# A graph network on one core: half groups, pieces of x by truncation, and blanking scatters moved up

## The chip, the cores and the metric

The kernel runs on one core of a Trainium2 chip. The metric is the device time of one execution, in microseconds (us). Before the change it is 10419.15 us, the median of three runs (10417.22 to 10422.83).

## The reference

Four graph networks run one after the other on the same graph of N = 6250 nodes and E = 106250 edges, with D = 128 features; after each of them x becomes layernorm(x + network(x)). `src` and `dst` are the two ends of the edges, in an order that is known only at run time.

```
L0, 4 layers: agg = segment_sum(x[src], dst); h = (1+eps)*x + agg; linear, batchnorm, relu, ...; x = h + x_in
L1:           segment_sum(x[dst] @ W_T + edge_attr_64 @ T, src); relu(x @ W_S + that)
L2, 4 layers: msg = relu(x[src] + silu(edge_attr_16 @ We)); agg = segment_sum(msg, dst); mlp; layernorm
L3:           score = exp(clip(sum_heads(K[src]*Q[dst]*(edge_attr_128 @ WE)))); segment sums of V[src]*score and score by dst
```

So nine times a row of x is fetched for every edge and summed per target node, and once keys and values are. Everything is float32.

## The kernel before

**Order of the edges.** The 6250 nodes are 50 tiles of 125. Edges are sorted on the chip by the pair (tile of dst, tile of src). Four edges of one pair are a unit, 128 units of one tile are a group, and there are `GROUPS` = 272 groups (34 `TRIPS` of `Q` = 8). A tile's last group is filled up with blank units. `buckets` makes the histogram and the tables of where each pair starts, `scatter` writes the record of every edge (`rec`, 328 words) to its place in DRAM with indirect DMAs of POOL (L701), `metadata` reads back the node numbers and gives every unit its partner place in the order by the other end (L713, one indirect DMA for each group).

**Blanking.** In `setup` SP writes blank records over the part of `rec` that may stay unused (L532), then in `prepare` over the last group of each of 51 tiles (L548). Only after these have landed does POOL blank the last unit of each pair with 50 indirect DMAs (L688), and only after those does the main loop of `scatter` begin (L701).

**An edge pass** (`edges`, nine times: four of kind "sum", one "attr", four "msg") has two stages. In the row stage TensorE fetches the row of x of each edge as a product with a one-hot matrix. A group has 512 edges and one tile of nodes, whose place in SBUF is loaded into a register. x is held as three bfloat16 pieces, whose sum is x, so that a group takes 4 x 3 matmuls of 128 columns (L827). The registers are loaded eight at a time (L500), once for each trip:

```
at_ = tiles_of(PE_E, nat_row, i * Q, Q)
...
for j in range(UNIT):
    for k in range(3):
        ins = pe.matmul(ps[:, r, c], hots_t[0:NT, r, c],
                        big16[0:NT, ds(at_[q] + (2 * HT + k) * NODES_PAD, D)], ...)
```

DVE makes the one-hot matrix (L1481), ACT evicts the 512 rows (L1082), SP stores them in DRAM in unit order (L613). In the sum stage POOL gathers the 128 units of a group of the other order (L729, an indirect DMA), DVE makes another one-hot matrix (L1519), TensorE multiplies (L848, four products in float32, each of which is two matmul instructions in the profile; L851 are those of the 66 further features of "attr"), and DVE adds the result to the target tile of x (L1533, L1536), whose place is again a register loaded at the start of the trip. In a "msg" pass DVE adds the edge term to the gathered rows (L1526) and ACT applies relu (L1110) in between. Rings of four or eight buffers and semaphores order all of it.

**Pieces of x.** At the start of each pass ACT rounds x to bfloat16 (L1096), DVE subtracts (L1495), ACT rounds the rest (L1099), DVE subtracts again (L1498), in four parts; TensorE waits for all.

**Attention** (`attn`): POOL gathers keys and values with four indirect DMAs for each group (L739), TensorE fetches the rows of Q (L862) and makes the segment sums (L870), DVE multiplies and adds.

Between the passes stand the stages `linear`, `norm_linear`, `norm_apply`, `norm_out`, `layer_norm`, `to_t` and others, which are matmuls or transposes over 25 blocks of 250 nodes. Each stage begins when the one before has raised `stage_done`.

## Time and profile before

| what | value |
|---|---|
| median of the runs | 10419.15 us |
| profiled execution: its own time, its span | 10417.13 us, 10415.4 us |
| busy TensorE matmul, weight load | 7541.2 us (72%), 6497.3 us (62%) |
| busy VectorE (DVE) | 7092.3 us (68%) |
| busy GpSimd (POOL) | 4975.9 us (48%) |
| busy ScalarE (ACT) | 3677.0 us (35%) |
| DMA bytes, mean rate | 2371.77 MB, 228 GB/s |
| TensorE clock granted, mean | 0.817 |

The span runs from the first to the last instruction, the device time also has what lies around it (1.7 us here). Busy time is the union of an engine's instructions. Instructions of the engines' sequencers (register arithmetic, branches, waits, register loads, DMA issues) are not counted as busy; a "q" behind an engine's name marks them. A source line such as L827 is that of the kernel before. An idle time stands before the instruction that ended it, with what released it.

### The profile page before, as it was taken

The numbers are of one execution on the slowest core, as the hardware profiler recorded it, in microseconds if no ns is written. First come the engines' busy times: TensorE is split into PE (matmuls) and PEld (weight loads), VectorE is DVE, ScalarE is ACT, GpSimd is POOL, SyncE is SP. The second block draws the span as 40 slices with busy tenths as digits, with TensorE's granted clock in tenths as the row PEclk, the third lists the DMA queues.
The fourth block names the chain that finished last, engine by engine and source line by source line (L and its number), as shares of the span: only waits on it lengthen the run. The fifth ranks groups of instructions, "written<-read, shape, count | busy, mean of one in ns | idle before, by whom it ended". The sixth has DMA issues, their size and how long they took to land.

```text
span 10415.4 us, 240438 instructions
## 1 busy us (share of the span) xinstructions
PE 7541.2 (72%) x64204; PEld 6497.3 (62%) x64205; DVE 7092.3 (68%) x16971; ACT 3677.0 (35%) x7598; POOL 4975.9 (48%) x4705
## 2 busy tenths in 40 slices
PE   4799990388786886883689778777776885666664
PEld 3467660277675775773589776666765765555553
DVE  5577770366766766666556589789798797666664
ACT  0122220230612504304520454644645644444443
POOL 0777776336064072370035137056074173777772
PEclk7555555699898998996899899899898998666665
DMA  8766665997584874960699489598696894666666
GB/s 339 199 211 210 212 211 31 111 293 219 212 288 119 324 242 153 330 188 13 174 325 384 188 330 366 208 345 308 252 356 232 322 366 161 161 164 160 164 160 79
DMA packets 1747196, 2371.77 MB, mean 228 GB/s; under 512 B 516388, under 2 KB 1046151, under 8 KB 1746651
## 3 DMA queue, kind: packets, MB, share of 16 engines
q1 hardware_dynamic: 1292446, 1275.33, 39.0%
q0 software_dynamic: 318912, 1049.17, 31.2%
q10 hardware_dynamic: 135677, 45.42, 1.9%
q8 instruction: 65, 1.06, 0.0%
q14 instruction: 96, 0.79, 0.0%
HBM read 1485.10 MB, written 955.49 MB: 234 GB/s over the span
## 4 chain that ended last, share of the span: by engine, by line
PE 19%; DVE 9%; POOL 7%; issue 7%; ACT 4%; DMA 3%; SPq 2%; DVEq 2%; ACTq 0%; POOLq 0%
PE ps L848 8%; PE ps L827 7%; POOL big L739 7%; DVE gath L1526 3%; ACT gath L1110 3%; DMA big<-kv_table,src_at 2%; PE ps L851 2%; SPq L613 2%; ACT big L1245 1%; DVE onehot L1481 1%; DVE heads L1599 1%; DVE gath L1595 1%; ACT gath L1082 0%; DVE gath L1610 0%; PE ps L977 0%
## 5 line engine op out<-in xcount | busy, mean ns | idle before, releaser
L729 POOL DMA_INDIRECT gath<-msg_units,unit_at_d x2176 | 2329.4, 1071 | 3263.2 <-DMA msg_units<-gath 2579.2
L848 PE MATMUL ps<-onehot,gath 128*128 128x125 f32 x18224 | 2585.0, 287 | 620.6 <-ACT gath L1110 347.4
L848 PEld LDWEIGHTS ps<-onehot,gath 128*128 128x128 f32 x18224 | 2219.4, 193 | 977.3 <-issue 528.0
L827 PE MATMUL ps<-big,onehot 125*128 x29376 | 1795.4, 221 | 862.3 <-DVE onehot L1481 694.8
L827 PEld LDWEIGHTS ps<-big,onehot 125*128 125x128 bf16 x29376 | 1695.3, 98 | 965.3 <-issue 934.0
L1082 ACT ACTIVATE gath<-ps 128x512 f32<-128x512 f32 x2448 | 1393.2, 596 | 726.0 <-PE ps L827 571.5
L1519 DVE TENSOR_TENSOR onehot<-iota,node_d 128x500 f32<-128x500 f32 x2176 | 1464.4, 673 | 169.2 <-PE ps L848 109.9
L1481 DVE TENSOR_SCALAR onehot<-row_b,part 125x512 bf16<-125x512 uint8 x2448 | 1129.5, 482 | 606.4 <-PE ps L827 582.9
L739 POOL DMA_INDIRECT big<-kv_table,src_at x1088 | 1094.1, 1006 | 532.2 <-issue 295.6
L701 POOL DMA_INDIRECT rec<-big,idx_ring x832 | 974.5, 1171 | 279.9 <-issue 241.2
L1533 DVE TENSOR_TENSOR big<-big,ps 128x125 f32 x2448 | 685.4, 280 | 546.7 <-PE ps L848 375.8
L1110 ACT ACTIVATE gath<-gath 128x512 f32<-128x512 f32 x1088 | 685.5, 630 | 933.5 <-DVE gath L1526 933.5
L862 PE MATMUL ps<-big,weights 125*128 x2176 | 463.6, 380 | 414.8 <-DVE weights L1572 414.7
L1161 ACT ACTIVATE big<-ps,feats 128x250 f32 x125 | 54.2, 470 | 1987.7 <-PE ps L917 1987.7
L1526 DVE TENSOR_TENSOR gath<-gath,big 128x512 f32<-128x512 f32 x1088 | 742.3, 683 | 15.6 <-DMA gath<-msg_units,unit_at_d 15.6
L862 PEld LDWEIGHTS ps<-big,weights 125*128 125x128 f32 x2176 | 402.0, 276 | 478.4 <-issue 478.3
L870 PE MATMUL ps<-gath,onehot 128*125 128x136 f32 x2176 | 503.9, 401 | 122.2 <-DVE gath L1610 111.2
L1120 ACT ACTIVATE onehot<-iota,weights 128x125 f32<-128x125 f32 x1088 | 344.7, 388 | 650.7 <-PE ps L870 606.5
L1589 DVE TENSOR_TENSOR gath<-big,ps 128x512 f32<-128x512 f32 x272 | 186.9, 687 | 537.2 <-DMA big<-kv_table,src_at 531.3
L870 PEld LDWEIGHTS ps<-gath,onehot 128*125 128x125 f32 x2176 | 439.0, 288 | 181.4 <-issue 134.7
L729 POOL DMA_INDIRECT big<-rec,unit_at_s x136 | 131.1, 964 | 753.6 <-DMA rec<-gath 651.2
L807 PE MATMUL ps<-weights,big 128*128 128x128 f32 x1664 | 422.0, 433 | 93.9 <-ACT big L1044 82.5
(223 smaller groups left out, 9121.9 us busy)
## 6 DMA issues: line engine op xcount, KB each, us to landing
msg_units<-gath SPq DMA_DIRECT2D x2176, 256.0 KB, 2.3
big<-ea_units SPq DMA_DIRECT2D x1088, 256.0 KB
ea_units<-rec SPq DMA_DIRECT2D x16, 4352.0 KB, 53.2
rec<-gath SPq DMA_DIRECT2D x272, 256.0 KB, 6.2
big<-rec SPq DMA_DIRECT2D x272, 256.0 KB
big<-in_attr_t SPq DMA_DIRECT2D x208, 256.0 KB
rec<-big SPq DMA_DIRECT2D x1, 43296.0 KB, 152.4
gath<-msg_units,unit_at_d POOLq DMA_INDIRECT x2176, 5.3
```

What stands on the lines that cost most here:

```text
L701: pool.indirect_dma_start(rec, bass.IndirectOffsetOnAxis(ap=idx_ring[:, q, k:k + 1], axis=0), rec_r[:, q, k, :], None).then_inc(rec_out[q] ...
L729: pool.indirect_dma_start(att_slot(q) if way == "attr" else gath[:, q, :], None, units, bass.IndirectOffsetOnAxis(ap=unit_at[w][:, g:g + 1 ...
L739: pool.indirect_dma_start(kv_r[:, q, k, :], None, table["kv"], bass.IndirectOffsetOnAxis(ap=src_at[:, g * PER + k:g * PER + k + 1], axis=0))\
L827: ins = pe.matmul(ps[:, r, c], hots_t[0:NT, r, c], big16[0:NT, ds(at_[q] + (2 * HT + k) * NODES_PAD, D)], start=k == 0, stop=k == 2)
L848: ins = pe.matmul(ps[:, RING + r, 0:NT], x, hots[:, r, j, :], start=j == 0, stop=j == UNIT - 1)
L862: last = pe.matmul(ps[:, 6 + q % 2, k * P:(k + 1) * P], oht_r[0:NT, q % 2, k, :], big[0:NT, ds(at_ + RE * NODES_PAD, P)], start=True, stop ...
L870: last = pe.matmul(ps[0:NT, q, 0:SUMS_W], hots[:, q, k, :], vs_r[:, q, k, :], start=k == 0, stop=k == PER - 1)
L1082: act.activation(unit_ring[:, q, :, :], ps[:, q % RING, :].rearrange("p (k f) -> p k f", f=D), ACT.Copy).then_inc(evicted, 1)
L1110: act.activation(gath[:, q, :], gath[:, q, :], ACT.Relu).then_inc(msg_ready, 1)
L1481: dve.tensor_scalar(hots_t[0:NT, r, :].rearrange("p (j u) -> p j u", u=P), row_b[0:NT, k, q % RING * GSLOTS:(q % RING + 1) * GSLOTS] .rear ...
L1519: dve.tensor_tensor(hots[:, r, :, :], iota[:, 0:NT].unsqueeze(1).to_broadcast([P, UNIT, NT]), node[w][:, ds(g * UNIT, UNIT)].unsqueeze(2). ...
L1526: dve.tensor_tensor(gath[:, q, :], gath[:, q, :], ea_r[:, q, :], ALU.add).then_inc(msg_sum, 1)
```

## The change

Three things change at once.

**Half groups.** A group still has 128 units, but it is now made of two halves of 64 units (`HALF`), and each half has a tile of its own. Filling up to 64 instead of 128 leaves 248 groups (31 trips) for 272. Each group therefore has two tile numbers: register loads take 16 values for 8, the row matmuls take their tile by half, the sums of the two halves are separate matmuls of 64 rows into separate banks, and DVE adds twice, the second time after the first add has ended (`half_added`). In the "attr" pass the product is turned round (nodes on the partitions, 194 columns), so `to_t` is needed twice behind it. The order of the slots within a group changes too, so that stores go out as two runs for each unit pair, and `attn_prep` permutes two tables with matmuls.

**Pieces of x by truncation.** The upper two bytes of each float32 word are used in place as a bfloat16, with a step of two elements (`upper`). DVE makes the two rests by subtraction in five parts, and does it inside the stages that make x (`norm_out`, `layer_norm`); only the first pass cuts at its own start. ACT takes no part.

**Blanking.** POOL's 50 scatters now wait for the first blanking transfer alone, and for the transfers to the last (now half) groups only before the main loop. Blank units that fall into those go to spare rows.

```diff
-GROUPS = ((E + (UNIT - 1) * NTILES * NTILES) // UNIT + NTILES * (P - 1)) // P + 1
+HALF = P // 2
+HALVES = ((E + (UNIT - 1) * NTILES * NTILES) // UNIT + NTILES * (HALF - 1)) // HALF + 1
-TRIPS = -(-GROUPS // (2 * Q)) * 2
+TRIPS = -(-HALVES // (2 * Q))
...
+        def without_upper(dve, src, dst, k):
+            src, dst = (slice(b + k * FIFTH_W, b + (k + 1) * FIFTH_W) for b in (src, dst))
+            return dve.tensor_tensor(big[0:NT, dst], big[0:NT, src], upper[0:NT, src], ALU.subtract)
+        def cut(dve, src, k):
+            without_upper(dve, src * NODES_PAD, REST, k).then_inc(rest_made, 1)
+            cuts[0] += 1
+            dve.wait_ge(rest_made, cuts[0])
+            without_upper(dve, REST, LOW, k).then_inc(low_cut, 1)
@@ SP, prepare @@
-                    sp.dma_start(rec_units[ds(c, P), :], blank.rearrange("p j w -> p (j w)")).then_inc(last_blank, 16)
+                    sp.dma_start(rec_units[ds(c, HALF), :], blank[0:HALF, :, :].rearrange("p j w -> p (j w)"))\
+                      .then_inc(last_blank, 16)
@@ POOL, scatter @@
-                pool.wait_ge(last_blank, 16 * BKT)
+                pool.wait_ge(tail_blank, 16)
...
                 pool.wait_ge(unit_blank, 16 * NTILES)
+                pool.wait_ge(last_blank, 16 * BKT)
@@ TensorE, row stage @@
-                    at_ = tiles_of(PE_E, nat_row, i * Q, Q)
+                    at_ = tiles_of(PE_E, nat_row, i * (2 * Q), 2 * Q)
                         for j in range(UNIT):
-                            for k in range(3):
-                                ins = pe.matmul(ps[:, r, c], hots_t[0:NT, r, c],
-                                                big16[0:NT, ds(at_[q] + (2 * HT + k) * NODES_PAD, D)],
+                            for b in (NA * NODES_PAD, REST, LOW):
+                                ins = pe.matmul(ps[:, r, c], hots_t[0:NT, r, c], upper[0:NT, ds(at_[2 * q + j // 2] + b, D)],
                 laps(pe, TRIPS, rows_of)
+                pe.wait_ge(evicted, base + GROUPS)
@@ TensorE, sum stage @@
                         for j in range(UNIT):
+                            for h in range(2):
+                                p = slice(h * HALF, (h + 1) * HALF)
+                                if way == "attr":
+                                    x = att_slot(q)[p, j * REC + AT_EA:j * REC + AT_EA + D + AX]
+                                    ins = pe.matmul(ps[0:NT, (1 - h) * RING + r, 0:D + AX], hots[p, r, j, :], x, ...)
+                                else:
+                                    ins = pe.matmul(ps[:, (1 - h) * RING + r, 0:NT], unit_ring[p, q, j, :], hots[p, r, j, :], ...)
@@ DVE, sum stage @@
-                    at_ = tiles_of(DVE_E, sum_row, i * Q, Q)
+                    at_ = tiles_of(DVE_E, sum_row, i * (2 * Q), 2 * Q)
                             one_hots(g + 2, (q + 2) % RING, first and q < 2)
+                        add(g, 0, q % RING, at_[2 * q], first and q == 0)
                             message(i + (q + 2) // Q, (q + 2) % Q)
-                        add(g, q % RING, at_[q], first and q == 0)
+                        add(g, 1, q % RING, at_[2 * q + 1], False)
@@ DVE, layer_norm (norm_out alike, one sweep late) @@
                     last.then_inc(ln_fifth, 1)
+                    if then_cut:
+                        dve.wait_ge(ln_fifth, 5 * n["scaled"] + i + 1)
+                        cut(dve, b, i)
@@ the network behind the attr pass @@
+    do("to_t", AC, D, 0, RE)
+    do("to_t", HT, D, 0, AC)
```

## Rows read from the trace of the kernel before

**Rows 1.** The page's chain that ended last, shares of the span by line.
```profile
PE ps L848 8%; PE ps L827 7%; POOL big L739 7%; DVE gath L1526 3%; ACT gath L1110 3%; DMA big<-kv_table,src_at 2%; PE ps L851 2%; SPq L613 2%; ACT big L1245 1%; DVE onehot L1481 1%; DVE heads L1599 1%; DVE gath L1595 1%; ACT gath L1082 0%; DVE gath L1610 0%; PE ps L977 0%
```

**Rows 2.** Stages: length; PE, PEld, DVE, ACT, POOL busy; clock, DMA share, GB/s.
```profile
161.50:257.00 95.50, 0.00 (x0) 0.00 (x0) 0.62 (x2) 0.00 (x0) 0.00 (x0) 0.50 0.99 364
257.60:351.00 93.40, 31.19 (x122) 22.14 (x119) 22.43 (x74) 5.97 (x15) 51.89 (x50) 0.52 0.84 181
...
1991.00:2215.50 224.50, 195.00 (x3264) 186.78 (x3264) 161.60 (x406) 153.60 (x272) 0.00 (x0) 0.99 0.84 316
2219.00:2582.60 363.60, 304.42 (x2176) 264.96 (x2176) 238.28 (x545) 0.00 (x0) 275.48 (x272) 0.98 0.91 246
5024.70:5307.60 282.90, 234.73 (x3264) 199.60 (x3264) 164.05 (x405) 160.16 (x269) 0.00 (x0) 0.98 0.88 247
5321.00:5802.70 481.70, 478.64 (x4352) 478.23 (x4352) 290.28 (x817) 0.00 (x0) 259.92 (x270) 0.99 0.98 379
6148.00:6542.00 394.00, 315.86 (x2176) 265.89 (x2176) 378.94 (x812) 170.76 (x271) 301.29 (x270) 0.99 0.98 356
8831.60:10303.00 1471.40, 951.20 (x4316) 829.68 (x4317) 913.14 (x1886) 592.43 (x1630) 1093.72 (x1088) 0.68 0.66 157
```

**Rows 3.** Sequencer of TensorE in one trip of the row stage, by line.
```profile
L821 PEldq ALU_OP  x8: 32/32/36, 2064.9 to 2069.2; - x8
...
L823 PEldq EVENT_SEMAPHORE  x5: 51/51/51, 2066.8 to 2069.3; - x5
L823 PEldq ALU_OP  x3: 32/32/32, 2065.0 to 2066.2; - x3
...
L827 PEldq FUSED_REGOPS  x24: 46/46/46, 2065.1 to 2069.7; - x24
```

**Rows 4.** Register loads: count, ns min/median/max, first and last start, in four stretches.
```profile
L500 PEldq TENSOR_LOAD <-tile_at x24: 1123/1142/1168, 2044.0 to 2195.6; - x24
...
L500 DVEq TENSOR_LOAD <-tile_at x26: 595/599/615, 6210.7 to 6497.2; - x26
...
L500 PEldq TENSOR_LOAD <-tile_at x34: 1478/1938/1964, 8839.8 to 10257.8; - x34
...
L500 PEldq TENSOR_LOAD <-tile_at x2: 551/1258/1964, 8831.4 to 8839.8; - x2
```

**Rows 5.** POOL's indirect DMAs: a sum stage, attention.
```profile
L729 POOL DMA_INDIRECT gath<-msg_units,unit_at_d x272: 942/949/1455, 2219.7 to 2577.3; - x136
...
L739 POOL DMA_INDIRECT big<-kv_table,src_at x1088: 941/947/1477, 8831.6 to 10302.1; - x182
```

**Rows 6.** Timeline of DVE within a trip of a "msg" sum stage.
```profile
6307.24 0.27 DVE L1533 TENSOR_TENSOR big<-big,ps 128x125 f32 x1
...
6307.43 0.67 DVE L1519 TENSOR_TENSOR onehot<-iota,node_d 128x500 f32<-128x500 f32 x1
6308.02 0.68 DVE L1526 TENSOR_TENSOR gath<-gath,big 128x512 f32<-128x512 f32 x1
...
6308.62 0.27 DVE L1533 TENSOR_TENSOR big<-big,ps 128x125 f32 x1
```

**Rows 7.** Sequencer of TensorE on line L862, in 37 groups of attention.
```profile
L862 PEldq FUSED_REGOPS  x37: 46/46/46, 9311.9 to 9498.1; - x37
```

**Rows 8.** Timeline of DVE where one trip of a sum stage ends.
```profile
3009.59 0.28 DVE L1533 TENSOR_TENSOR big<-big,ps 128x125 f32 x1 [0.41 <-PE ps L848]
...
3010.80 0.68 DVE L1519 TENSOR_TENSOR onehot<-iota,node_d 128x500 f32<-128x500 f32 x1 [0.93 <-issue]
```

**Rows 9.** Timeline from the end of a stage to its pass's first matmul.
```profile
2669.03 3.02 ACT L1096 ACTIVATE big<-big 125x1632 bf16<-125x1632 f32 x2
...
2686.63 2.67 PE L827 MATMUL ps<-big,onehot 125*128 x23 [18.15 <-DVE onehot L1481]
```

**Rows 10.** Groups by line: name, count, busy us, mean ns, idle before.
```profile
L1767 DVE TENSOR_TENSOR big<-big,rows 125x1280 f32<-125x1280 f32 x5 | 7.5, 1493 | 0.2
```

**Rows 11.** Transposes of two `to_t` stages, one behind the other.
```profile
L934 PE MATMUL ps<-ident,big x100: 270/322/442, 4885.2 to 4900.8; 125*128 125x125 f32 x100
```

More of the change, by code:

```diff
@@ L159, in network @@
     do("attend")
-    do("norm_out", RE, HT, ACT.Identity, None)
+    do("norm_out", RE, HT, ACT.Identity, False)
     do("layer_norm", NA, D, None, None, False, None, "out", False)
@@ L353, in program @@
         base_u = of_small([BKT, 2, BKT])
-        quad, some, blank_f = (of_small([BKT, BKT]) for _ in range(3))
+        quad, some, blank_f, spare = (of_small([BKT, BKT]) for _ in range(4))
         groups_of = of_small([BKT, 2])
@@ L475, in do @@
                     names.append("io")
-                if kind == "norm_out" and args[3] or kind == "layer_norm" and args[6]:
+                if kind == "layer_norm" and args[6]:
                     names.append("io_fifths")
@@ L719, in edges @@
                 base, laps_before = n["edges"] * GROUPS, n["edges"] * TRIPS
-                units = rec_units if way == "attr" else msg_units
+                units = rec_units[0:UNITS + P, :] if way == "attr" else msg_units
                 if w == "s":
@@ L885, in attn, with attn_prep @@
                 sums(GROUPS - 1, RING - 1)
+            def attn_prep(n):
+                pe.wait_ge(turns_made, 1)
+                for t, v in enumerate((node_f, src_f)):
+                    v = v.rearrange("p (g i j) -> p g i j", i=2, j=2)
+                    for h in range(2):
+                        for i in range(2):
+                            last = pe.matmul(ps[:, 2 * t + h, 0:2 * GROUPS], turns[:, 2 * h + i, :], v[:, :, i, :],
+                                             start=i == 0, stop=i == 1)
+                last.then_inc(turned_at, 1)
             def attend(n):
@@ L1074, in load_rows, with keep_rows @@
                                   .partition_broadcast(P // 32)).then_inc(row_in[k], 16)
-                def keep_rows(i, first, last):
-                    for h in range(2):
+                def keep_rows(i, first, last, trips=2):
+                    for h in range(trips):
                         for q in range(Q):
@@ L1467, in spread, with row_hots @@
                     dve.stream_shuffle(words, words, [0] * 32).then_inc(row_spread, 1)
-                def row_hots(i, first, last):
-                    for h in range(2):
+                def row_hots(i, first, last, trips=2):
+                    for h in range(trips):
                         for q in range(Q):
@@ L1581, in add @@
                     dve.wait_ge(attn_sums, g + 1)
-                    ch.wait()
-                    a = big[0:NT, ds(at_ + HT * NODES_PAD, SUMS_W)]
-                    ch.mark(dve.tensor_tensor(a, a, ps[0:NT, q, 0:SUMS_W], ALU.add))
+                    for h in range(2):
+                        ch.wait()
+                        a = big[0:NT, ds(at_[h] + HT * NODES_PAD, SUMS_W)]
+                        ch.mark(dve.tensor_tensor(a, a, ps[0:NT, q, h * SUMS_W:(h + 1) * SUMS_W], ALU.add))
                 def times_q(g, trip, q):
@@ L1592, in times_eh @@
                 def times_eh(trip, q):
[L1593 removed]
+                    dve.wait_ge(eh_in[q], 32 * trip)
                     sch.wait()
@@ L1692, in norm_linear, with norm_out, pieces @@
                 bn_finish(n, g, b)
-            def norm_out(n, src, dst, func, tab):
-                with dve.Fori(0, NBLK) as j:
-                    dve.wait_ge(act_blk, n["applied"] * NBLK + j + 1)
-                    x = T(XT)[:, ds(j * BLK, BLK)]
-                    dve.tensor_tensor(x, x, T(dst)[:, ds(j * BLK, BLK)], ALU.add).then_inc(added, 1)
+            def norm_out(n, src, dst, func, then_cut):
+                base = n["blocks"] * NBLK
+                def pieces(i):
+                    dve.wait_ge(mm_free, base + SLOTS_PS * (i + 1))
+                    cut(dve, NA, i)
+                for i in range(SWEEPS):
+                    for j in range(i * SLOTS_PS, (i + 1) * SLOTS_PS):
+                        dve.wait_ge(act_blk, n["applied"] * NBLK + j + 1)
+                        x = T(XT)[:, j * BLK:(j + 1) * BLK]
+                        dve.tensor_tensor(x, x, T(dst)[:, j * BLK:(j + 1) * BLK], ALU.add).then_inc(added, 1)
+                    if then_cut and i:
+                        pieces(i - 1)
+                if then_cut:
+                    pieces(SWEEPS - 1)
             def conv(n, l):
```

276 lines of the change are left out of this document (150 added, 126 removed).

## The prediction

> **What bounds the kernel now.** I read the chain of waits by line, which names no single bound [rows 1], then the stages one by one [rows 2], because each has its own limit. The reader is to see four kinds.
> - The row stage takes 224.5 us for 272 groups, eight times (the "attr" one 282.9) [rows 2]. TensorE is busy 195.0 us of it. What sets the pace is TensorE's sequencer. In a trip of 8 groups it carries out 8 + 8 + 24 register and wait instructions between 2064.9 and 2069.7 [rows 3]: 39 intervals in 4.8 us, 0.123 us each, with the 96 weight loads and 96 matmuls in between. It then branches and loads eight registers, which takes 1142 ns [rows 4]. The loads come every (2195.6 - 2044.0)/23 = 6.59 us [rows 4], and 34 x 6.59 is the whole stage. The matmuls alone need 195.0/34 = 5.7 us a trip.
> - The "sum" sum stages (363.6 us) go at POOL's pace: 271 intervals in 357.6 us, 1.32 us for each gather [rows 5]. So does attention, 1470.5/1087 = 1.353 us, four for each group [rows 5]; metadata is one such DMA for each group and little else.
> - The "msg" sum stages (394 us, DVE busy 379 [rows 2]) go at DVE's pace: add to one-hot 0.19 us, one-hot to message 0.59, message to add 0.60, in all 1.38 [rows 6], and (6497.2 - 6210.7)/25 = 11.46 us a trip [rows 4].
> - The "attr" sum stage has DMA share 0.98 at 379 GB/s and TensorE 478.6 of 481.7 us busy [rows 2]: both are full, with 4352 matmuls at 0.110 us.
>
> **The change part by part.** All sums are made against the profiled execution, 10417.13 us, 2.0 under the median of the runs; terms are rounded to 1 us.
>
> *Row stages.* Groups fall from 272 to 248, trips from 34 to 31. But the tile of slots 0 and 1 is no longer that of slots 2 and 3. In a trip there are 24 fused register instructions on the line of the matmuls [rows 3], one for each different address and not one for each of the 96 matmuls: three pieces x 8 groups. Attention's four products on one tile also have one for each group, 37 in 186 us [rows 7]. With two tiles a group has six addresses, so 24 more instructions a trip. At 0.123 us [rows 3] that is 2.95 us. Bounds: nothing, if the compiler reuses the registers, and 0.15 us each, 3.6 us. I take the measured mean, because the three that stand already are of the same kind in the same place. The load of 16 registers isn't in the trace. At an aligned start the number counts little: two cost 551 ns on TensorE, eight cost 599 on DVE [rows 4]. Bounds are nothing and, with attention's 8 at a shifted start for 1938 ns, 0.24 us for each, 16 x 0.24 - 1.14 = 2.7 us [rows 4]. I take one more short access, 0.55 us. Trip: 6.59 + 2.95 + 0.55 = 10.09 us; stage: 31 x 10.09 = 313 us, 88 more than 224.5, eight times: +704. "attr": 313 for 282.9 us, +30. DVE (161.6 busy) and ACT (153.6) stay under that [rows 2]. The stores have twice the runs at half the length; with a DMA share of 0.84 now and a slower pace they are covered. The rows of x are read with a step of four bytes: bounds nothing and, as with the float32 passes at 0.110 us against 195.0/3264 = 0.060 [rows 2], 12 x 0.11 = 1.32 us a group, 10.6 us a trip, 0.5 over the sequencer's 10.09 (+140 in nine stages). I take nothing. TensorE's new wait for the last eviction has the sum stage behind it, which waits for the stores of the same rows: nothing.
>
> *"sum" sum stages.* POOL: 248 x 1.32 = 327 us. DVE in a trip: eight one-hots to first add, 0.60 each, eight first adds to second, which wait for the end of the first (0.28 and some 0.08 for the release), seven second adds to the next one-hot at 0.19, and the end of the trip, now 1.21 us [rows 8], with 0.55 more for the load: 4.8 + 2.9 + 1.4 + 1.8 = 10.9 us, 337 us for 31. That is a little more than POOL's, so DVE takes the bound: with the 5 us that the stage has around the gathers 342 us, -22 each, -88.
> The matmuls are 16 of 64 rows where 8 of 128 rows stand, alternating between the upper and the lower half of the array and between two banks. If the halves run side by side, TensorE needs what it needs now, 304.4/272 = 1.12 us a group [rows 2]. No row shows two such halves; the bound on the other side is one after the other, 16 x 0.110 = 1.76 us a group (rival 2). I take side by side, since nothing in the operands ties one half to the other. The Trainium skill (TensorEngine Tiling (Array Packing), Key Properties) says that tiles of the array load weights and multiply in parallel, which leaves the sum as it is; no trace here shows it.
>
> *"msg" sum stages.* The first add moves between one-hot and message, where its end is hidden, so it costs its issue, 0.19 us [rows 6]: a trip is 11.46 + 8 x 0.19 + 0.55 = 13.5 us, 31 are 419 us, +25 against 394, four times: +100. The fewer groups don't pay for the second add.
>
> *"attr" sum stage.* DMA-bound: each group gathers the same bytes, 481.7 x 248/272 = 439, -42. TensorE: 8 passes of 194 columns at 0.110 x 194/125 = 0.171, 1.37 us a group, if the halves run side by side.
>
> *Attention.* POOL-bound: 24 x 4 x 1.353 us = -130. DVE's busy 913 of 1471 us covers the second add (248 x 0.3) and the longer load. SP has one more issue a group, with 5.4 us for three. *Metadata:* at the same price 24 x 1.353 = -32.
>
> *Pieces of x.* Before each pass 17.6 us go by from the stage's end to the first matmul [rows 9]. Afterwards two subtractions of 1280 columns stand there, 1.49 us each [rows 10], then the spreading and the first one-hots. But the cuts weigh on DVE in the stages before: 10 x 1.49 = 15 us. In `norm_out` and in `layer_norm` with weights DVE gets full and gives some back: -8 (three) and -12 (three); without weights it is idle enough: -15 and -17. The first pass keeps its cut: -1. Together -93. Without the cover it would be 8 x 17.6 less 8 x 15, -21.
>
> *Blanking.* The transfers of the last groups take 95.5 us, the scatters 93.4 us behind them [rows 2]. Side by side, with half the bytes in the first (at 364 GB/s 47 us), the scatters start at 161.5 and end after 93 us at best and 93 + 47 at worst. POOL's issue takes 66 of the 93, so part of the others' bytes fits in: I take 107, which is -83 (bounds -97 and -49).
>
> *New stages.* Two `to_t`, of the size of those that take 15.6 us and their eviction now [rows 11]: +16. The permutation in `attn_prep`: 16 float32 passes of 496 columns, 0.110 x 496/125 = 0.44 us, and four copies: 7 + 3 us, and up to twice the first at the clock of 0.50 that TensorE has after idling, as at 161.5 us [rows 2]: +13 with a wait.
>
> **Sum.** +704 + 30 - 88 + 100 - 42 - 130 - 32 - 93 - 83 + 16 + 13 = +395, so 10417 + 395 = 10812, and 10815 as a run's time.
>
> **Rivals.**
> 1. *Faster: the addresses cost nothing.* The compiler or the queue of TensorE hides the 24 added instructions. For it: the matmuls need only 5.7 of the 6.59 us. Against it: the sequencer's instructions fill the trip without a gap [rows 3]. The rows would take 31 x 6.59 = 204 us (-20 each, "attr" -25): 10417 - 339 - 185 = 9893; with the 0.55 us for the load 10047. It decides where the nine row stages lose less than the other terms gain, 339/9 = 38 us: below (224.5 + 38)/31 = 8.47 us a trip.
> 2. *Slower still: the half matmuls queue.* 1.76 us a group. The "sum" stages take 248 x 1.76 + 5 = 441 (+99 on my 342, four times), "msg" 441 (+22, four times), "attr" 16 x 0.171 = 2.73 us, 678 (+239): 10812 + 723 = 11535. For it: the "attr" stage now shows 16 passes a group at just this pace. Against it: those fill all 128 rows.
> 3. *Slower still: each loaded register costs 0.24 us*, as at the shifted starts [rows 4]. Rows: 2.15 us more a trip, 31 x 9 times, 600. DVE: 16 x 0.24 - 0.60 - 0.55 = 2.7 us a trip, 31 x 8 times, 670. That is 12080. Against it: the aligned loads of eight. The Trainium skill (Runtime: NRT & Kernel Launch, Instruction fetch mechanics) has some 200 ns for each register even in bulk; attention's loads agree (0.24 us), the aligned ones don't (599 ns for eight).
>
> **How the numbers follow.** Forecast 0.56, rival 1 0.20, rival 2 0.16, rival 3 0.08. The forecast's own range is 10400 to 11250: below, 0.095 us an instruction and no price for the load; above, 0.15 us, the load doubled and the step of four bytes paid. Over all cases 9900 to 11500 holds rival 1 and part of rival 2, and leaves out 0.08 + 0.10. Faster by over 0.2% (about 21 us, what a measurement of this kernel can tell): 0.20 and the low end of the forecast, 0.23. Within it: 0.03. Slower: 0.74.
>
> **What would show it.** Row stage: 48 fused register instructions a trip on the line of the matmuls, trips of some 10.1 us for 6.59, TensorE waiting for its sequencer; rival 1 has 24 of them or 6.6 us. Sum stage: matmuls of the two halves starting together, 342 us for 363.6; rival 2 has 0.11 us between all starts. Loads of 16: near 1.7 us on TensorE, or 3.8. "msg": DVE full, 13.5 us a trip. Attention: 1341 us. First scatter at 162 us, main loop at 268. First matmul of a pass 4 to 9 us behind the stage. Wrong as a whole is the prediction if the row stages come out under 262 us each.

## The result

The changed kernel takes 11272.36 us, the median of four runs (11264.59 to 11281.23), where the kernel before takes 10418.18 on the same chip: a ratio of 1.082, 95% interval 1.0807 to 1.0833. It is slower by 854 us. I had forecast slower by 396; the forecast's own range ended at 11250, the one over all cases at 11500. The sign and several of the mechanisms were right, the size was less than half of it.

I read the stages first, since each has its own limit. This is the view by stages of the changed kernel, with the columns of [rows 2]: the blanking scatters; the blanking that was still to land; a "sum" row stage and its sum stage; the "attr" row and sum stages; a "msg" sum stage; attention.
```profile
164.10:225.00 60.90, 0.00 (x0) 0.00 (x0) 0.00 (x0) 0.00 (x0) 45.72 (x50) 0.50 0.99 175
225.00:348.50 123.50, 10.53 (x43) 8.45 (x44) 9.54 (x31) 2.99 (x6) 0.00 (x0) 0.50 0.82 176
2734.10:3064.90 330.80, 269.54 (x2976) 232.78 (x2976) 155.09 (x369) 147.45 (x247) 0.00 (x0) 0.83 0.56 196
3068.50:3430.90 362.40, 291.00 (x3968) 252.11 (x3968) 270.23 (x745) 0.00 (x0) 235.48 (x248) 0.95 0.78 225
5343.60:5728.40 384.80, 287.24 (x2976) 240.74 (x2976) 161.18 (x370) 148.13 (x248) 0.00 (x0) 0.82 0.55 166
5737.00:6163.80 426.80, 372.11 (x3969) 319.88 (x3969) 336.50 (x1241) 0.00 (x0) 236.92 (x248) 0.99 0.98 391
6616.00:7073.90 457.90, 323.65 (x3968) 281.21 (x3968) 398.50 (x989) 155.96 (x248) 245.72 (x246) 0.89 0.88 279
9827.00:11153.00 1326.00, 852.56 (x3931) 744.26 (x3932) 899.97 (x1959) 540.21 (x1486) 977.81 (x992) 0.68 0.67 159
```
TensorE and DVE are both busy for a smaller share in the row and msg stages than before: neither is full, so something between their instructions has grown. The granted clock has fallen with it: 0.99 of full speed in a row stage before [rows 2], 0.83 now, which is 2.4 GHz for two thirds of the time and 1.2 for the rest, while the pause at the end of a trip has grown from 0.90 to 1.93 us (below).

The terms of my sum against the two profiled executions (span 10415.4 and 11266.5 us), each measured from matmul to matmul of the stages, so that nothing is left over:

| term | forecast | measured |
|---|---|---|
| eight row stages | +704 | +849 |
| "attr" row stage | +30 | +97 |
| four "sum" sum stages | -88 | -14 |
| four "msg" sum stages | +100 | +233 |
| "attr" sum stage | -42 | -56 |
| pieces of x, with the two `to_t` | -77 | -88 |
| blanking, up to the end of the scatter | -83 | -1 |
| metadata | -32 | -40 |
| attention and the rest | -117 | -129 |
| sum | +395 | +851 |

**A row trip.** The timeline of TensorE in a row stage, first before, then changed; a line is a run of matmuls without a gap, and in brackets stands the pause ahead of it.
```profile
2099.80 4.07 PE L827 MATMUL ps<-big,onehot 125*128 x70
2104.77 5.70 PE L827 MATMUL ps<-big,onehot 125*128 x96 [0.90 <-ACT gath L1082]
```
```profile
2099.71 5.69 PE L858 MATMUL ps<-big,onehot 125*128 x66
2107.29 8.76 PE L858 MATMUL ps<-big,onehot 125*128 x96 [1.89 <-issue]
2117.98 6.20 PE L858 MATMUL ps<-big,onehot 125*128 x68 [1.93 <-issue]
```
The 96 matmuls of a trip are one line, and in the pause ahead of it stands the register load. So a trip is 5.70 + 0.90 before and 8.76 + 1.93 now. Both parts have grown. These are the loads at the ends of the same trips, before and then changed (the first of each starts at 2103.3 and at 2105.5):
```profile
L500 PEldq TENSOR_LOAD <-tile_at x2: 1140/1144/1147, 2103.3 to 2109.9; - x2
```
```profile
L515 PEldq TENSOR_LOAD <-tile_at x2: 1413/1415/1417, 2105.5 to 2116.1; - x2
```
Before, the load started 0.6 us ahead of the end of the last matmul (2099.80 + 4.07 = 2103.87), so that half of it was covered. Now it starts 0.1 us behind that end (2099.71 + 5.69 = 2105.40), and all of it stands in the pause. The load itself is only 0.27 us longer.

The sequencer's instructions of one such trip, and the register loads of the row stage and of a msg sum stage, in the changed kernel:
```profile
L852 PEldq ALU_OP  x7: 32/32/32, 2011.9 to 2018.3; - x7
```
```profile
L858 PEldq FUSED_REGOPS  x48: 64/64/64, 2011.0 to 2019.3; - x48
```
```profile
L515 PEldq TENSOR_LOAD <-tile_at x26: 1404/1425/2436, 1997.5 to 2266.7; - x26
```
```profile
L515 DVEq TENSOR_LOAD <-tile_at x31: 1096/1101/1124, 6618.7 to 7056.8; - x31
```
**Where a msg trip ends.** The timeline of DVE in the changed kernel, to hold against [rows 6]:
```profile
6690.83 0.28 DVE L1576 TENSOR_TENSOR big<-big,ps 128x125 f32 x1
6691.02 0.68 DVE L1560 TENSOR_TENSOR gath<-gath,big 128x512 f32<-128x512 f32 x1
6691.63 0.28 DVE L1576 TENSOR_TENSOR big<-big,ps 128x125 f32 x1
6693.12 0.68 DVE L1553 TENSOR_TENSOR onehot<-iota,node_d 128x500 f32<-128x500 f32 x1 [1.22 <-issue]
```
Inside a trip a group takes 1.58 us, 0.20 more than before, which is the 0.19 of the forecast. At the end of the trip DVE stands still for 1.22 us, and TensorE then has no work for 1.7 us. In most trips one slow group of matmuls follows, here the first of the second line (timeline of TensorE, same stage):
```profile
6680.70 1.16 PE L883 MATMUL ps<-onehot,gath 64*128 64x125 f32 x16 [1.73 <-DVE onehot L1553]
6682.28 3.44 PE L883 MATMUL ps<-onehot,gath 64*128 64x125 f32 x32 [0.42 <-ACT gath L1147]
6686.11 1.16 PE L883 MATMUL ps<-onehot,gath 64*128 64x125 f32 x16 [0.39 <-ACT gath L1147]
```
A group is 16 half matmuls in 1.16 us, and two groups 1.58 us apart should end 2.7 us after the first one's start, not 3.44. The first took 1.80 us at a granted clock of 0.50, which is 1.2 GHz, the group ahead of it 1.16 us at 0.97 (the same columns as above):
```profile
6680.70:6681.90 1.20, 1.16 (x16) 0.97 (x16) 1.20 (x4) 0.38 (x1) 0.81 (x1) 0.97 0.78 215
6682.30:6684.10 1.80, 1.80 (x16) 1.80 (x18) 1.55 (x4) 0.63 (x1) 0.79 (x1) 0.50 0.85 241
```
DVE then waited 0.65 us for it. Trips without such a group take 14.0 us, the others 14.7. The 1.16 us also settle rival 2: 16 half matmuls one behind the other at 0.110 us would take 1.76. In the trace the matmuls of the two halves start in pairs, 0.007 us apart, and the pairs every 0.111 us.

**The "attr" row stage.** What the engines waited for in it (total us, times, longest):
```profile
DVE onehot L1520 <- PE ps L858: 217.2, 200, 3.2
ACT gath L1124 <- DMA rec<-gath: 206.7, 208, 2.5
PEld ps L858 <- issue: 116.4, 122, 2.3
```
ACT waits for the landing of stores, at a DMA share of 0.55. The stores aren't slow (2.2 us from issue to landing): SP issues them late, two a group at 0.80 us each, one behind the other, since a half group's rows to `rec` need a transfer of their own. That is 12.85 us a trip, which the stage shows from its seventh trip on; the first ones take 10.7, as in the other row stages.

### The profile page after: what moved, and what is told of

Its sections match the earlier page's. It is cut to its first block, busy times and chain, and to the rows that moved or that the text cites. A ratio compares the mean times of both kernels' runs of the same rounds, so it can differ in the third digit from the quotient of the medians.

```text
span 11266.5 us, 268085 instructions
## 1 busy us (share of the span) xinstructions
PE 7933.5 (70%) x75296; PEld 6635.5 (59%) x75297; DVE 7279.9 (65%) x18698; ACT 3412.1 (30%) x7120; POOL 4463.7 (40%) x4369
## 4 chain that ended last, share of the span: by engine, by line
PE 18%; DVE 9%; issue 9%; POOL 6%; ACT 3%; SPq 3%; DMA 3%; DVEq 2%; ACTq 0%; POOLq 0%
PE ps L858 10%; POOL big L770 6%; PE ps L883 6%; SPq L639 3%; DVE gath L1560 2%; ACT gath L1147 2%; DVE big L1576 2%; DMA big<-kv_table,src_at 2%; DVEq L515 1%; DVE big L1572 1%; ACT gath L1124 1%; DVE onehot L1553 1%; DVE big L1573 1%; ACT big L1279 0%; DMA big<-rec 0%
## 5 line engine op out<-in xcount | busy, mean ns | idle before, releaser
L760 POOL DMA_INDIRECT gath<-msg_units,unit_at_d x1984 | 1985.8, 1001 | 4585.0 <-DMA msg_units<-gath 3404.1
L858 PE MATMUL ps<-big,onehot 125*128 x26784 | 2441.3, 250 | 1000.2 <-issue 495.1
L883 PE MATMUL ps<-onehot,gath 64*128 64x125 f32 x31744 | 2430.5, 300 | 886.7 <-DVE onehot L1553 421.8
L858 PEld LDWEIGHTS ps<-big,onehot 125*128 125x128 bf16 x26784 | 2093.3, 112 | 1351.1 <-issue 1076.3
L883 PEld LDWEIGHTS ps<-onehot,gath 64*128 64x128 f32 x31744 | 2104.6, 203 | 1212.5 <-issue 439.5
L1553 DVE TENSOR_TENSOR onehot<-iota,node_d 128x500 f32<-128x500 f32 x1984 | 1338.3, 675 | 314.6 <-PE ps L883 238.5
L1576 DVE TENSOR_TENSOR big<-big,ps 128x125 f32 x3968 | 1107.8, 279 | 249.6 <-PE ps L883 104.7
L770 POOL DMA_INDIRECT big<-kv_table,src_at x992 | 977.8, 986 | 528.3 <-issue 278.7
L1560 DVE TENSOR_TENSOR gath<-gath,big 128x512 f32<-128x512 f32 x992 | 679.6, 685 | 27.0 <-DMA big<-ea_units 19.2
L1506 DVE STREAM_SHUFFLE row_b<-row_b 128x512 int32<-128x512 int32 x558 | 406.8, 729 | 0.0
```

What stands on the lines that cost most here:

```text
L760: pool.indirect_dma_start(att_slot(q) if way == "attr" else gath[:, q, :], None, units, bass.IndirectOffsetOnAxis(ap=unit_at[w][:, g:g + 1 ...
L770: pool.indirect_dma_start(kv_r[:, q, k, :], None, table["kv"], bass.IndirectOffsetOnAxis(ap=src_at[:, g * PER + k:g * PER + k + 1], axis=0))\
L858: ins = pe.matmul(ps[:, r, c], hots_t[0:NT, r, c], upper[0:NT, ds(at_[2 * q + j // 2] + b, D)], start=b == NA * NODES_PAD, stop=b == LOW)
L883: ins = pe.matmul(ps[:, (1 - h) * RING + r, 0:NT], unit_ring[p, q, j, :], hots[p, r, j, :], start=j == 0, stop=j == UNIT - 1)
L1553: dve.tensor_tensor(hots[:, r, :, :], iota[:, 0:NT].unsqueeze(1).to_broadcast([P, UNIT, NT]), node[w][:, ds(g * UNIT, UNIT)].unsqueeze(2). ...
L1560: dve.tensor_tensor(gath[:, q, :], gath[:, q, :], ea_r[:, q, :], ALU.add).then_inc(msg_sum, 1)
```

## The experiments

Two of the four chips of these runs have slower POOL transfers, for every kernel alike (the kernel before takes 10401 and 10408 us on two, 11130 and 11222 on the others), so each ratio is against the kernel before on its own chip, and across chips I compare only the row stages, which hold no POOL transfer: the kernel before has them at 223 to 226 us on both kinds (e12). e1, e5, e9 and e12 are single executions.

### One tile for both halves (e1)

```diff
-at_ = tiles_of(PE_E, nat_row, i * (2 * Q), 2 * Q)      # DVE's sum stage alike
+at_ = tiles_of(PE_E, nat_row, i * Q, Q)
-... upper[0:NT, ds(at_[2 * q + j // 2] + b, D)]
+... upper[0:NT, ds(at_[q] + b, D)]
```

> Left out: the second half of a group takes the tile of another group, in the row stages and in the adds, so that a trip loads 8 registers for 16 and a group has 3 addresses for 6; all matmuls, adds and transfers stay. Theory (the sequencer's address instructions and the register loads set the time): per group of a row stage 3 fused register instructions at 0.143 us apart and 0.2 us for the rest, 0.63 to 0.66 us, with 1.85 us at the end of the trip some 7.1 us a trip for 10.72, so a row stage of 220 us for 331. In the msg sum stages the idle time of DVE at the end of a trip falls from 1.22 to some 0.3 us and with it TensorE's slow group goes (clock back over 0.97): 8 x 1.58 + 0.4 = 13.1 us a trip for 14.7, 406 us for 456. The sum sum stages go from 359 to about 332 us, where POOL's gathers (1.32 us) take over. Rival (the rows of x read at a step of four bytes, or TensorE's lower clock, set the pace): the row trip stays above 9.5 us. Rival for the sum stages (the second add's wait itself costs): msg trip stays above 14.2 us.

Measured: 10251.16 us, where the kernel before takes 10408.33 there. Row stages 222 to 243 us, msg sum stages 421 us, sum sum stages 331 us, a msg trip 13.3 us. That is 157 us under the kernel before, where the change is 854 over it: the loads and the second half's addresses together cost the change some 1010 us, and without them it would be a gain. The step of four bytes and the wait of the second add stay in this run, so they are not the cause of the loss. The run doesn't part the loads from the addresses. The "attr" row stage stayed at 380.1 us: it isn't paced by addresses.

### Three-step addresses (e2)

```diff
-dve.tensor_scalar(tiles_i[:, 2:4, :], ..., float(D), ...)
+dve.tensor_scalar(tiles_i[:, 2:4, :], ..., float(2 * D), ...)
-upper[0:NT, ds(at_[...] + b, D)]
+big16[0:NT, ds(at_[...] + (2 * b + 1), 2 * D)].rearrange("p (d t) -> p d t", t=2)[:, :, 0]
```

> The tile addresses are kept doubled in the table, so that a fused register instruction of the row stage holds three steps (add, multiply, add) for five; their number stays 48 a trip. Theory (the sequencer sets the row stages): each instruction takes 46 ns for 64 and they stand 0.124 us apart for 0.143, so a trip takes 10.72 - 48 x 0.019 = 9.8 us, a row stage 304 us for 331, eight of them -216 us; the attr one stays near 380 (another limit). Total near 11055 us. Rival (the step of four bytes or the clock of 0.84 sets the pace of the matmuls): row trip within 0.1 of 10.7, total 11270.

Measured: 11147.55 us, ratio 1.0713 (1.0682 to 1.0744). The instructions went to 46 ns and the matmuls of a trip to 7.89 us, but the pause grew, so that a row stage came to 313 to 317 us and not 304. From the same timeline and the list of register loads:
```profile
2106.48 7.89 PE L859 MATMUL ps<-big,onehot 125*128 x96 [2.33 <-issue]
```
```profile
L516 PEldq TENSOR_LOAD <-tile_at x30: 1397/1870/2411, 1949.0 to 2247.0; - x30
```
The same load now takes 1.87 us for 1.43: it isn't a fixed price, and half of what the addresses gave it took back. The granted clock was 0.84, as in the changed kernel (0.83), and the matmuls of a trip still took 0.87 us less: in this stage the sequencer sets the pace, not the lower clock.

### Blanking from 128 partitions (e3)

```diff
-sp.dma_start(rec_units[ds(c, HALF), :], blank[0:HALF, :, :].rearrange("p j w -> p (j w)"))
+sp.dma_start(rec[ds(c * UNIT, HALF * UNIT), :].rearrange("(p j) w -> p (j w)", j=2),
+             blank[:, 0:2, :].rearrange("p j w -> p (j w)"))
```

> The blanking of the last half groups writes the same bytes from 128 partitions of SBUF (two records each) and not from 64 (four records each). Theory (a transfer out of 64 partitions gets about half the rate: 17.1 MB at some 180 GB/s here, where full groups went at 364 GB/s before): the engines' time is 47 us for these and some 80 to 93 for the scatters, so the main loop of the scatter starts at 290 to 305 us for 336, -30 to -45 us of the whole. Rival (many writes beside scatters, or writes to DRAM as such, go at 180 GB/s whatever the source): it starts within 5 us of 336.

Measured: 11215.42 us, ratio 1.0778 (1.0747 to 1.081). The main loop of the scatter starts at 319.7 us for 348.5 (the 336 of the expectation was the first work of the other engines; POOL itself started later), so 29 us come from here; of the other 28 us of the difference 10 stand in the kernel before too (10408 us on this chip for 10418), and the rest is spread over the stages. The bytes up to that start are the same, 32.4 MB, and took 156 us for 184. SP's transfers, in the changed kernel and then here:
```profile
L571 SPq DMA_DIRECT2D rec<-big x51: 502/720/7255, 164.8 to 330.2; - x51
```
```profile
L571 SPq DMA_DIRECT2D rec<-big x51: 348/349/3322, 164.0 to 302.1; - x51
```
The last were issued at 330.2 and 302.1 us: same bytes, another source. Each partition also gives two records in one piece here, for four, which the run doesn't tell apart from the number of partitions.

### The second store by ACT, and one store a group (e4, e5)

```diff
 # e4, in ACT's eviction of "attr"
+act.wait_ge(evicted, base + g + 1)
+act.dma_start(slots_of(g, 1, AT_EA), triple_ring[:, q, 1, :, :]).then_inc(stored[q], 16)
 # e5, in SP, for the two stores
+sp.dma_start(rec[ds(g * GSLOTS, GSLOTS), AT_EA:AT_EA + D].rearrange("(p j) w -> p j w", j=UNIT), unit_ring[:, q, :, :])
```

> In the attr row stage the store of the second half of a group is issued by ACT behind its eviction, not by SP. Theory (SP's issues set the pace there: two a group, 0.80 us each, 12.85 us a trip): the stage falls from 380 us to the 331 to 340 of the other row stages, since ACT needs 0.6 + 0.1 + 0.55 us of the 1.34 of a group; whole time -40 to -50. Rival (the transfers of short runs themselves are the limit, or the landing of the stores that ACT waits for): 370 us or more.

> The changed kernel with one store a group in the attr row stage for two, the same 256 KB in runs of four records for two; the rows of the second half land in places of the old order, so the pairing of rows and nodes in that pass is left out. Theory (SP's two issues a group, 0.80 us each, set the stage, not the bytes and not ACT): the attr row stage falls from 380 us to the 331 to 340 of the other row stages. Rival (the bytes to records that lie 1312 bytes apart are the limit, as 283 us for 224 before suggests): 360 us or more.

Measured: e4 11281.52 us (ratio 1.0842, 1.081 to 1.0873), the stage at 425 us, longer than the 380. That is the mark that I had given to the rival, but the experiment was a bad one: on ACT eviction, the wait for its end and the issue come one behind the other, at least 1.57 us a group and 1.78 in the mean (14.0 to 14.5 us a trip), so that ACT itself probably became the bound, and it decided nothing. e5 took 11195.69 us, where the kernel before takes 10401.25, and the stage 349.9 us, so one issue a group gives back 30 us. Its runs in DRAM are also twice as long; what speaks for the issues is that in the changed kernel SP sends one store behind the other, 0.80 us apart, and so sets the 12.85 us of a trip. The stage stayed above the expected 331 to 340, and what holds the last 10 to 20 us there I haven't found.

### Pieces of x alone, three and five steps (e6, e7)

The cuts, `norm_out` and `layer_norm` of the change on the kernel before, with whole groups and 8 registers a trip; e6 has the doubled addresses of e2, e7 those of the change.

> The kernel before with the pieces of x by truncation alone, and with doubled tile addresses so that a fused register instruction keeps three steps. Theory: the gaps before the passes shrink as in the changed kernel (104 to 93.5 three times, 354 to 338, 108 to 94, 83 to 69.5 three times, 29 to 25), -105 us in all, and the row stages stay at 224 to 226, since neither the step of four bytes nor anything else in them is new: 10310 us. Rival (reading bf16 at a step of four bytes slows the matmuls): row stages of 235 us and more, 10390 us or above.

> The same with the address written as in the change, so that a fused register instruction holds five steps. Theory: 24 of them a trip, 0.019 us more each, 0.46 us a trip and 15 us a row stage, eight times, and little in the attr one: 125 us more than with three steps, 10430 us, about what the cuts save. Rival (only the number of the instructions counts): the same time as with three steps.

Measured: e6 10354.15 us, ratio 0.9951 (0.9934 to 0.9968); e7 10403.62, ratio 1.0001 (0.9992 to 1.0011). The gaps shrank as expected, by 114 us in all. But a row stage takes 229 to 230 us for 224 to 226 in e6, and 236 in e7. A "sum" row stage of the kernel before (from e12, below), of e6 and of e7, as in [rows 2]:
```profile
2862.10:3087.50 225.40, 194.91 (x3264) 186.96 (x3264) 161.30 (x405) 152.60 (x271) 0.00 (x0) 0.99 0.84 315
```
```profile
2672.90:2902.20 229.30, 208.55 (x3264) 200.31 (x3264) 162.21 (x405) 156.25 (x271) 0.00 (x0) 0.99 0.83 310
```
```profile
2670.10:2905.60 235.50, 209.28 (x3264) 199.75 (x3264) 162.32 (x405) 156.31 (x271) 0.00 (x0) 0.99 0.81 302
```
The same 3264 matmuls are busy 208.6 us for 194.9: reading bf16 at a step of four bytes costs 4 ns a matmul, some 5 us a stage. The other address form, at the same count of 24 a trip, costs another 6.5, less than the 15 expected; I take it that with three addresses a group the sequencer has some slack, as the 4.8 us of its instructions beside 5.70 us of matmuls suggest. As they stand in the change, the cuts are worth nothing.

### Blanking alone (e8)

The wait of POOL and the spare rows of the change, on the kernel before.

> The kernel before with the scatters of the blank units beside the last-group transfers alone. Theory (the 16 DMA engines are full in both, 95.5 us at 364 GB/s and 93 at 181): side by side the sum of their busy time, 95 + 78 = 173 us, is the floor, so the main loop starts at 335 us for 351, -10 to -20 us in all. Rival (they hide behind each other, as the prediction had it): start at 300 us or below, -50 us. Second rival (they hinder each other): no gain or a loss.

Measured: 10415.81 us, ratio 1.0013 (1.0003 to 1.0023): no gain, if anything a loss; the main loop starts at 357 us for 351. The two stretches from POOL's first scatter to that start:
```profile
163.30:223.10 59.80, 0.00 (x0) 0.00 (x0) 0.00 (x0) 0.00 (x0) 44.86 (x50) 0.50 1.00 256
223.10:357.00 133.90, 10.45 (x43) 8.43 (x44) 10.76 (x35) 2.99 (x6) 0.87 (x1) 0.50 0.81 259
```
That is 50.0 MB in 193.7 us; one behind the other it was 95.5 us at 364 GB/s and 93.4 at 181, 51.7 MB in 188.9 [rows 2]. The shares were 0.99 and 0.84 one behind the other, so there was little to overlap. Even that little was not won: the busy times add up to 173 us, which is where the 335 us of the expectation came from, and side by side it took 194. The second rival of the expectation, that the two hinder each other, fits best; how they do is open.

### Loads and addresses apart (e9, e10, e13), and the kernel before again (e12)

```diff
 # e9, the changed kernel: 16 registers, 3 addresses
-upper[0:NT, ds(at_[2 * q + j // 2] + b, D)]
+upper[0:NT, ds(at_[2 * q] + b, D)]
 # e10, the kernel before: row trips of 16 groups
-at_ = tiles_of(PE_E, nat_row, i * Q, Q)
-for q in range(Q):
+at_ = tiles_of(PE_E, nat_row, i * (2 * Q), 2 * Q)
+for q in range(2 * Q):
 # e13, the kernel before: load 16, use 8 (TensorE's rows and DVE's sums)
-at_ = tiles_of(PE_E, nat_row, i * Q, Q)
+at_ = tiles_of(PE_E, nat_row, i * Q, Q if last else 2 * Q)
```

> The changed kernel; in the row stages a trip still loads 16 registers, but all four products of a group use the first half's tile, so it has 24 addresses a trip for 48; the rows of second halves from another tile are left out, the sum stages stay whole. If the addresses carry the loss: 8 groups of 0.63 to 0.66 us and 2.2 to 2.4 us at the end of a trip (the load of 16 at 1.4 to 1.9 us and the branch), 7.4 to 7.7 us a trip, a row stage of 230 to 239 us, near the 222 to 236 of the run with 8 loaded registers. Rival (the load of 16 carries it): 9 us a trip and more, 280 us. The msg sum stages stay at 445 to 458 us, since DVE still loads 16.

> The kernel before with row trips of 16 groups on TensorE: one load of 16 registers for two of 8, nothing else. Theory (addresses, branch and register load of TensorE's sequencer set the row stage): 16 x 0.60 + 0.5 + 1.4 to 1.9 = 11.5 to 12 us for 16 groups where two trips take 13.2, so 17 of them 196 to 204 us, but the matmuls alone are busy 195; stage 203 to 212 us for 224, eight times, -100 to -170 us in all; the attr row stage stays. Rival (the matmuls, ACT or the stores already hold it, the load is hidden): 220 us or more.

> The kernel before once more, to have its stage times from the chip of the next two runs: row stages 224 to 226 us, sum sum stages 354 to 358 and msg ones 391 to 394, unless POOL's transfers are slower on this chip, as on the last one (the sum stages 400 us there in kernels that change only the row stage).

> The kernel before, but each trip loads 16 registers and uses the first 8, on TensorE in the row stages and on DVE in the sum stages (the last trip loads 8). Nothing else changes, addresses are the same. Theory (half of the loss is the load): the time in which TensorE has no matmul at the end of a trip grows from 0.90 us to between 1.45 and 2.4, so a trip takes 7.15 to 8.1 us and a row stage 243 to 275 us; DVE's pause in a msg trip grows from 0.28 to 1.2 us, so these stages take 420 to 430 us for 394; 300 to 500 us in all. Rival (the load hides behind the matmuls that are still queued, as my prediction's 0.55 us had it): row stages of 240 us at most and msg stages under 405, +150 us.

Measured: e9 11475.29 us against 11129.85, row stages 274 to 285 us, which is what the rival named (280 us), not the theory (230 to 239). e10 11191.94 us, ratio 1.0057 (1.004 to 1.0073), row stages 226 to 233. e12 11235.51 us. e13 11584.7 us against 11222.32, ratio 1.0323 (1.0306 to 1.0341), row stages 263 to 270 for the 223 to 226 of e12. Trips on TensorE in e13, then in e10:
```profile
2205.17 7.32 PE L827 MATMUL ps<-big,onehot 125*128 x96 [1.87 <-issue]
2213.55 5.67 PE L827 MATMUL ps<-big,onehot 125*128 x96 [1.07 <-ACT gath L1082]
```
```profile
2202.89 11.03 PE L827 MATMUL ps<-big,onehot 125*128 x192 [2.40 <-issue]
2216.41 11.03 PE L827 MATMUL ps<-big,onehot 125*128 x192 [2.49 <-issue]
```
and the loads of e12, e13 and e10:
```profile
L500 PEldq TENSOR_LOAD <-tile_at x30: 1128/1152/1497, 2125.0 to 2316.5; - x30
```
```profile
L500 PEldq TENSOR_LOAD <-tile_at x31: 1373/2102/2682, 2123.7 to 2359.3; - x31
```
```profile
L500 PEldq TENSOR_LOAD <-tile_at x15: 1842/2722/2793, 2090.5 to 2281.3; - x15
```
Eight unused registers in the load cost 41 us a row stage: 329 of the 362 us of e13, and 23 more are the "attr" one's. Not all of that is pause. These are a row stage of e13 and two of its trips, with the columns of [rows 2]; e12's stage stands above:
```profile
2902.10:3172.40 270.30, 212.84 (x3264) 204.83 (x3264) 163.59 (x405) 154.85 (x271) 0.00 (x0) 0.92 0.70 263
2925.60:2933.10 7.50, 7.29 (x96) 7.07 (x96) 4.41 (x11) 4.16 (x8) 0.00 (x0) 0.77 0.61 225
2934.00:2939.90 5.90, 5.67 (x96) 5.44 (x96) 4.30 (x12) 3.98 (x8) 0.00 (x0) 1.00 0.77 291
```
The same 3264 matmuls are busy 212.84 us for 194.91, since behind the longer pauses some trips run in part at 1.2 GHz: 18 of the 45 us that this stage lost are the clock's, 27 the pauses'. So on the kernel before the load alone costs much: 225 us a row stage, 266 with the load of 16, 278 in e9 (its stage has 31 trips for 34, read at a step and with five-step addresses), 331 with the second addresses. No run has the second addresses with loads of 8, so how the two share the loss when they come together isn't shown. My theory for e10 fell: one load of 16 and the pause round it (2.4 us) cost more than two of 8 (2 x 0.90). The msg stages of e13 say nothing, since POOL's transfers held them on that chip (434 to 436 us in e12 already); for DVE the load's price rests on e1, where the msg trip went from 14.7 to 13.3 us.

### Two mixtures (e11, e14)

> Pieces of x by truncation with three-step addresses, and row trips of 16 groups, both on the kernel before. The two effects should add: 47 us of the first as measured, and the second limited by matmuls that take 0.0631 us each when they read at a step of four bytes (12 x 272 of them are 206 us): row stages of 208 to 214 us for 230, 10190 to 10230 us in all. Rival (the step of four bytes eats the second gain): 10300 us or more.

> The changed kernel with three-step addresses and with blanking of the last half groups from 128 partitions. Both were measured alone at -125 and -57 us, and touch different stages, so they should add: 11272 - 180 = 11090 us, still 670 above the kernel before. If the first one's gain came from the chip's spread rather than from the row stages, the sum falls short by 50 us or more.

e11 is e6 with the wide trips of e10: 11069.31 us, ratio 0.9937 (0.992 to 0.9953). That is 61 us under the kernel before on its chip, where the expectation had some 170 to 210 (row stages of 208 to 214). The second gain wasn't there to add, as e10 shows, though at the slower matmuls wide trips do no harm: row stages of 227 to 229. Its interval overlaps that of e6, so either is the best version I have, 0.5 to 0.6% under the kernel before. e14 is e2 with e3: 11858.36 us against 11222.32, 636 us more, ratio 1.057 (1.0553 to 1.0588), where 670 were expected; its row stages take 313 to 317 us, as in e2.

## Why the prediction was wrong

Right were: 48 fused instructions for 24, the halves side by side (rival 2 is out), the second add at 0.19 us in a msg group, POOL's price in attention (1.336 us a transfer) and metadata, the pieces' gain in the gaps, and that the row stages would decide. Rival 1 is out: the row trip took 10.7 us, not 6.6; e1, with neither the loads nor the second addresses, gives about what it would have been worth, 10251 us. Rival 3, each register 0.24 us, is out: 16 took 1.10 us on DVE and 1.43 on TensorE.

What failed, by size:
- **The end of a trip, with the load of 16 registers** ("I take one more short access, 0.55 us"). The pause of TensorE's trips grew by 1.03 us (0.90 to 1.93) and that of DVE's msg trips by 0.95 (0.27 to 1.22). The 0.48 us too little are 119 of the 145 us that I missed in the eight row stages; with 0.40 us in the msg and some 0.4 in the sum trips it is 215 us in all. On TensorE it was not the load's own length that I had too short: that grew by 0.27 us. My sum kept the overlap that stood there, where the load started 0.6 us ahead of the last matmul's end. With 48 longer instructions the sequencer is the slower of the two, the engine has run out of matmuls when the load comes, 0.1 us after that end, and this lost cover is 0.67 of the 1.03 us. On DVE the load itself grew from 0.60 to 1.10 us, 0.06 us a register, and e1, with 8 registers, had a pause of 0.56: so 0.66 of the 0.95 go with the load, and 0.29 with something else in the half groups that no run here isolates. The rows at hand had misled me: on DVE 8 registers took 599 ns, and I took two on TensorE at 551 as proof that the number counts little. My bounds, nothing to 2.7, held it.
- **The reading of the row trip as full of sequencer work.** The 4.8 us of instructions lie beside 5.70 us of matmuls; what bounded a trip before were the matmuls and the pause. The added 2.95 us came out near 8.76 - 5.70 = 3.06 all the same, because two errors met: the sequencer had 0.9 us of slack to use up, and its instructions became longer (0.143 us for 0.123, 0.96 us over the 48). That the sum came near here is luck. I had bounded that duration at 0.15 and taken 0.123, as being "of the same kind"; they were not, at a step of two elements.
- **"msg": what a pause does to the clock.** The slow group at a clock of 0.50, 0.7 us in most trips, some 70 us in the four stages, was not in the sum at all. With the pause cut to 0.56 us (e1) the clock was back at 1.00 and all trips alike.
- **"attr" rows: SP's issues** (+97 for +30). I had weighed the stores by DMA share, not by issues: two of 0.80 us a group where one stood. Of the 67 us missed, e5 gives back 30; 18 more are those by which every row stage came out over my 313 (331), and the rest is open.
- **Blanking** (-1 for -83). My lower bound was -49. I let two groups of transfers pass beside each other although [rows 2] gives their DMA shares as 0.99 and 0.84: work that fills the same 16 engines adds up, and in e8 it took 194 us where the sum of the busy times was 173. I also took half the bytes for half the time; out of 64 partitions they and the scatters went at 176 GB/s, where the transfers of whole groups had 364 [rows 2].
- **"sum" sum stages** (-14 for -88): a trip of 11.3 us for my 10.9, by the pause, and some 11 us around the 31 trips for my 5.

That is 215 + 27 (addresses, 0.11 us a row trip) + 70 + 67 + 82 = 461 us, out of 501 by which five terms came out dearer; the other four were 45 us better than I had them. Of the 67 some 20 stay unexplained, and so do the 40 us between 461 and 501.

The Trainium skill (Runtime: NRT & Kernel Launch, Instruction fetch mechanics) has some 200 ns for each register of a load even in bulk. DVE's loads here grow by 63 ns a register, so the measurement decides. The Trainium skill (TensorEngine Tiling (Array Packing), Key Properties) says that tiles of the array can load weights and multiply in parallel. The trace agrees, with 16 half matmuls in 1.16 us.

## What to carry to other kernels

Before a loop gets a second dynamic address, count three things apart: the address instructions of the sequencer and how long each is; the load of the registers, of which the 0.6 us that matmuls had covered stood open here once the sequencer was the slower of the two; and what the pause does to the clock of the engine that waits. Two streams of transfers that each nearly filled the DMA engines gained nothing side by side here; add their busy shares first, and take the sum as the least. And split a change into its parts on the chip: of this one's three the cuts were worth 0.5% with another address form and nothing as written, the blanking nothing, and what is left, the half groups, carries all of the loss.

## What was new of the hardware

- A register load of TensorE had no fixed price. Eight registers took 1.15 us behind matmuls that ended 0.6 us after its start; 16 took 1.43 in the changed kernel, 1.87 with shorter addresses, 2.10 in e13 and 2.72 in e10. On DVE it was 0.60 and 1.10 throughout. What the spread on TensorE depends on stays open: it was longer in the runs where the sequencer was less held by addresses.
- A fused register instruction took 46 ns in the form of the kernel before and of e2, and 64 in that of the change (three and five steps, as I count them).
- In e13, where TensorE's pauses grew from about 1 to up to 2.4 us, some of the trips behind them ran at a mean granted clock of 0.77, and their 96 matmuls took 7.3 us for 5.7.
- bf16 read at a step of four bytes: 0.0639 us a matmul of 128 columns for 0.0597 (208.55 and 194.91 us over 3264).
- With writes to DRAM out of 64 partitions of SBUF the DMA engines moved 176 GB/s at a share of 0.82. With the same bytes out of 128 (and half as long a piece from each) it was 205 at a share of 0.68, beside the same scatters.
